# A graph-network kernel on one Trainium2 core: GpSimd's second sum of weights is moved ahead of the fifth unit of row gathers

## The chip, the cores and the metric

The kernel runs on one core of one Trainium2 chip. A core has five engines that run side by side and meet at semaphores: TensorE (PE in the profile; PEld is its weight load), VectorE (DVE), ScalarE (ACT), GpSimd (POOL) and SyncE (SP, which only issues DMAs). The metric is the device time of one execution in microseconds. Before the change it is 3512.61 us, the median of 3 runs (3510.88 to 3514.73).

## The reference, cut to what matters

The program is a graph network over 1250 nodes of 768 features: two attention layers, and then a relational layer with 34 relations and 41250 edges. The part that the change touches is the relational layer:

```
agg  = segment_sum(x[src], edge_type * n + dst)        # per relation and node
mean = agg / max(cnt, 1)
h1   = sum over r of mean[r] @ W_rel[r] + x @ W_root + b_rgcn
xw   = h1 @ W_gcn          # then one more sum over the edges, a bias, a layer norm
```

The kernel turns the order round: it first computes `y[r] = x @ W_rel[r]` for all relations, stores these rows in DRAM, and then gathers for each edge the row `y[type, src]`, scales it by 1/count and adds it up per destination node.

## The kernel before, in words

The output columns are computed in two halves of 384 (`q` is 0 or 1; the name `y_half` in the profile is the store in DRAM). In each half 17 steps go over two relations at a time. The products of a step are made by a scheme with seven block products in place of eight (`m1` to `m7`), for 5 tiles of nodes each: 35 slots of 9 f16 matmuls of 128x384 (lines L2424, L2426, L2427). It needs four sums of weight blocks in each step, all made on GpSimd from the loaded weights, each a TENSOR_TENSOR of 128x1152:

- the first (`t3`, L792): X1 = B22 - B12, as soon as the next step's weights have landed;
- the second (`t1`, L798): B12 = B12 - B11, in place, after VectorE has measured B11 and B12 (the wait on `w_max`);
- the third (`t2`, L800): X2 = B22 - B12, after the second;
- the fourth (`t4`, L806): B11 = B21 - X2, at the start of the next step, after VectorE's `low` of product 1 (L1799).

In the second half (`q` = 1) fifteen of the steps also sum the edges of the first half, six units of 512 edges a step, numbered 0 to 5. For each unit

- GpSimd's `gather` issues four indirect DMAs (L840) of 128 rows of y. They need the row buffers free, of which there are two sets, so unit c's gathers wait (`e_lo`) for VectorE's rows of unit c - 2, two of them at a time;
- ScalarE's `edge_high` (L1213) scales the four sets of rows and rounds them;
- VectorE's `edge_low` makes for each set a one-hot matrix (L1838) and the rest of the rounding (L1840);
- TensorE's `edge_sum` multiplies them (L2400, L2401, eight matmuls), and VectorE's `edge_add` (L1861) adds the result up.

Every engine's order within a step is written out by hand in its `one_step` or `rows_step`. TensorE runs m1, m7, unit 0, m6, m2, m5 (first tile), unit 1, the rest of m5, m4, m3, unit 2, then tiles 2 and 3 of m1 and m7 and tile 2 of m6, unit 3, tile 3 of m6, m2, the largest weight (`spread_max`), m5, m4, unit 4, m3, and tile 4 with unit 5. VectorE measures the next step's weights (L1764) just ahead of `edge_low` of unit 3, then stands `edge_add` of unit 2, then `edge_low` of unit 4, then the additions for m2 and `scale`. The outputs of the products leave PSUM by ScalarE (L1238) and VectorE (L1875).

On GpSimd a step of the loop (`rows_step`) is: fourth sum, gathers of units 1, 2, 3, first sum, gathers of units 4 and 5, second and third sum, gathers of unit 0 of the next step (in the code: unit `PER`). The loop runs 14 times, and a fifteenth step stands behind it without the last gathers.

Of the kernel before, what the change touches and what calls it, by code (L numbers as in the profile page):

```python
# [19 lines left out]
def program(nc, x, src, dst, etype, norm_g, norm_b, W1, a_src1, a_dst1, b1, W2, a_src2, a_dst2, b2,  # L20
# [32 lines left out]
    with ctx:  # L53
# [484 lines left out]
        def step(q, i):  # L538
            return i + q * PAIRS


        def unit(q, i, m, c):

            return i * m + (c + q * UNITS), c % 2, i * (m // 2) + (c // 2 + q * (UNITS // 2) + W_USES[0])
# [208 lines left out]
        def _(pool):  # L753
# [34 lines left out]
            def t3(q, i):  # L788

                for j in range(2):  # L790
                    pool.wait_ge(w_loaded[j], step(q, i) * 16 + 16)
                nc.gpsimd.tensor_tensor(X1, B22, B12, ALU.subtract).then_inc(t_done, 1)  # L792

            def t1_t2(q, i):

                pool.wait_ge(w_max, step(q, i) * 5 + 2)
                pool.wait_ge(t_done, step(q, i) * 4 + 1)
                nc.gpsimd.tensor_tensor(B12, B12, B11, ALU.subtract).then_inc(t_done, 1)  # L798
                pool.wait_ge(t_done, step(q, i) * 4 + 2)
                nc.gpsimd.tensor_tensor(X2, B22, B12, ALU.subtract).then_inc(t_done, 1)  # L800

            def t4(q, i):

                pool.wait_ge(w_lo_ready, step(q, i) * 7 + LOW[1])
                pool.wait_ge(t_done, step(q, i) * 4 + 3)
                nc.gpsimd.tensor_tensor(B11, B21, X2, ALU.subtract).then_inc(t_done, 1)  # L806
# [25 lines left out]
            def gather(q, i, m, c):  # L832

                V, place, _ = unit(q, i, m, c)
                pool.wait_ge(idx_next, V + 1)
                for t in range(UT):
                    if t % FREE == 0:
                        pool.wait_ge(e_lo, V * UT + (t + FREE))
                        pool.nop(nofuse=True)
                    nc.gpsimd.indirect_dma_start(  # L840
                        out=graw[place * UT + t], out_offset=None, in_=y_dram[q],
                        in_offset=bass.IndirectOffsetOnAxis(ap=idx_now[:, c % IDXB, t:t + 1], axis=0))\
                        .then_inc(g_loaded[place * UT + t], 16)
# [20 lines left out]
            pool.wait_ge(o2_ones, 1)  # L864
            t3(0, 0)
            t1_t2(0, 0)
            t4(0, 0)
            pool.wait_ge(idx_copied, 1)
# [6 lines left out]
            pool.wait_ge(x1_lo, 7 * HT)  # L875
            t3(0, 1)
            t1_t2(0, 1)

            def weights_step(q, i, next_q, next_i, b):

                t4(q, i)
                pool.wait_ge(idx_copied, i + 1)
                pool.nop(nofuse=True)
                weigh(b, 0)
                weigh(b, 1)
                t3(next_q, next_i)
                weigh(b, 2)
                weigh(b, 3)
                t1_t2(next_q, next_i)
                weigh(b, 4)  # L890
                weigh(b, 5)

            def rows_step(q, i, e, next_q, next_i, last=False):

                t4(q, i)
                gather(q - 1, e, PER, 1)
                gather(q - 1, e, PER, 2)
                gather(q - 1, e, PER, 3)
                t3(next_q, next_i)
                gather(q - 1, e, PER, 4)  # L900
                gather(q - 1, e, PER, 5)
                t1_t2(next_q, next_i)
                if not last:
                    gather(q - 1, e, PER, PER)

# [16 lines left out]
            with pool.Fori(0, AGG_PAIRS - 1) as i:  # L922
                rows_step(1, i + 1, i, 1, i + 2)
            rows_step(1, AGG_PAIRS, AGG_PAIRS - 1, 1, AGG_PAIRS + 1, True)
            plain_step(1, PAIRS - 1, HALVES, 0)
            t4(HALVES, 0)
# [1801 lines left out]
```

## Time and profile before

| What | us |
|---|---|
| Median of 3 runs | 3512.61 (3510.88 to 3514.73) |
| Span of the profiled execution, first to last instruction | 3486.4 |
| Median less span: what lies around the span | 26.2 |
| TensorE busy | 3187.3 (91% of the span) |
| VectorE busy | 2289.5 (66%) |
| GpSimd busy | 1672.5 (48%) |
| ScalarE busy | 1477.8 (42%) |
| The fifteen steps with row gathers, from fourth sum to fourth sum | 918.46 |

The profiled execution's time with what lies around its span is not told apart from the runs; the 26.2 us are taken for it. Busy time of TensorE is a union of modelled matmul times (0.33 us for a matmul that is started every 0.16 us), so a pause under 0.17 us does not show in it; the length of a step does.

### The profile page before, as it was taken

To read this page: it belongs to the slowest core of one execution; us is meant where nothing else is said; L and a number is where in the kernel's file an instruction comes from. 1 tells how busy PE (TensorE), PEld (TensorE's weight loads), DVE (VectorE), ACT (ScalarE), POOL (GpSimd) and SP (SyncE) were. 2 spreads that over 40 slices of the span, in tenths; PEclk is the share of its full clock that TensorE was granted. 3 is DMA by queue.
4 is the path that set the end of the run, shared out by engine and by line. 5 is a ranking of instruction groups with operands and counts; after the bars stand their busy time and mean duration, and the time that the engine had idled before them with its cause. 6 is when DMAs were issued, how large, how long until landed. Compare 5 with 4: busy or idle time off the path is not lost.

```text
span 3486.4 us, 59747 instructions
## 1 busy us (share of the span) xinstructions
PE 3187.3 (91%) x17307; PEld 1981.5 (57%) x17307; DVE 2289.5 (66%) x4661; ACT 1477.8 (42%) x2713; POOL 1672.5 (48%) x1373
## 2 busy tenths in 40 slices
PE   6989998987999999999999999999999998678888
PEld 4544458976555555555556666666666654333545
DVE  8989988869744544454556877878788754432335
ACT  3767757645433323233343545545455531110010
POOL 3720000003566666656414565665656536766653
PEclk9999999998999999999999999999999998889899
DMA  3020012021423233232335564555556534664442
GB/s 91 2 73 0 0 55 79 1 87 59 152 90 124 97 116 120 103 124 98 124 104 170 172 199 155 194 164 178 187 169 198 152 127 130 192 178 136 133 111 80
DMA packets 228626, 411.91 MB, mean 118 GB/s; under 512 B 37764, under 2 KB 177923, under 8 KB 228534
## 3 DMA queue, kind: packets, MB, share of 16 engines
q1 hardware_dynamic: 167664, 268.22, 21.9%
q0 software_dynamic: 60480, 142.01, 15.2%
q8 instruction: 54, 0.88, 0.1%
q10 hardware_dynamic: 390, 0.50, 0.1%
q14 instruction: 38, 0.31, 0.0%
HBM read 259.19 MB, written 151.32 MB: 118 GB/s over the span
## 4 chain that ended last, share of the span: by engine, by line
PE 71%; DVE 12%; issue 7%; POOL 3%; another core or an unknown queue 3%; ACT 2%; DVEq 1%; DMA 1%; ACTq 0%; POOLq 0%
PE bank L2427 17%; PE bank L2424 17%; PE bank L2426 16%; PE bank L2413 6%; POOL placed_dram L778 3%; DVE arena L1635 3%; PE bank L2266 2%; PE bank L2400 2%; PE bank L2401 2%; PE bank L2326 2%; PE bank L2671 2%; DVE arena L1692 2%; DVE arena L1730 2%; DVE arena L1634 1%
## 5 line engine op out<-in xcount | busy, mean ns | idle before, releaser
L2424 PE MATMUL bank<-arena 128*128 128x384 f16 x3675 | 1205.3, 328 | 59.5 <-ACT arena L1238 38.2
L2427 PE MATMUL bank<-arena 128*128 128x384 f16 x3675 | 1204.2, 328 | 6.3 <-issue 6.2
L2426 PE MATMUL bank<-arena 128*128 128x384 f16 x3675 | 1203.9, 328 | 4.7 <-issue 4.6
L1238 ACT ACTIVATE arena<-bank,winv 128x384 f32<-128x384 f32 x700 | 395.7, 578 | 973.1 <-PE bank L2427 813.3
L1875 DVE SCALAR_TENSOR_TENSOR arena<-bank,winv,arena 128x384 f32<-128x384 f32 x525 | 313.9, 613 | 399.0 <-PE bank L2427 362.3
L2424 PEld LDWEIGHTS bank<-arena 128*128 128x128 f16 x3675 | 360.9, 98 | 324.4 <-ACT arena L1238 46.2
L2427 PEld LDWEIGHTS bank<-arena 128*128 128x128 f16 x3675 | 361.0, 98 | 248.6 <-issue 13.8
L2426 PEld LDWEIGHTS bank<-arena 128*128 128x128 f16 x3675 | 361.4, 98 | 238.6 <-issue 14.9
L1799 DVE SCALAR_TENSOR_TENSOR arena<-arena,wscale 128x1152 f16<-128x1152 f32 x245 | 367.8, 1536 | 193.7 <-ACT arena L1171 177.3
L840 POOL DMA_INDIRECT arena<-y_half,idx_now x360 | 395.1, 1097 | 190.1 <-issue 101.9
L854 POOL DMA_INDIRECT arena<-y_half,idx_now x360 | 351.8, 977 | 185.1 <-issue 106.1
L2413 PE MATMUL bank<-arena 128*128 128x384 f32 x720 | 281.9, 539 | 70.5 <-issue 45.3
L1861 DVE TENSOR_TENSOR arena<-arena,bank 128x384 f32 x180 | 99.3, 552 | 299.6 <-remote 139.8
L1171 ACT ACTIVATE arena<-arena,wscale 128x1152 f16<-128x1152 f32 x245 | 294.9, 1245 | 1.9 <-DVE wscale L1786 1.5
L863 POOL MEMSET arena<- 1x1250 f32 x1 | 1.1, 1136 | 604.9 <-DVE arena L1715 604.9
L1213 ACT ACTIVATE agg_hi<-arena,typ_s 128x384 fp32r<-128x384 f32 x360 | 192.4, 607 | 171.4 <-PE bank L2401 151.6
L2413 PEld LDWEIGHTS bank<-arena 128*128 128x128 f32 x720 | 145.8, 210 | 192.3 <-issue 101.9
L1840 DVE SCALAR_TENSOR_TENSOR agg_lo<-arena,typ_s,agg_hi 128x384 fp32r<-128x384 f32 x360 | 237.9, 661 | 12.5 <-ACT agg_hi L1213 10.2
L2212 PE MATMUL bank<-arena 128*128 128x512 f16 (+1 forms) x1080 | 212.9, 346 | 25.0 <-DVE arena L1635 18.4
L806 POOL TENSOR_TENSOR arena<-arena 128x1152 f32<-128x1152 f32 x35 | 92.2, 2634 | 292.7 <-DVE arena L1799 292.7
L827 POOL DMA_INDIRECT w_now<-rel_inv_dram,idx_now x192 | 198.9, 1036 | 54.7 <-issue 51.5
L792 POOL TENSOR_TENSOR arena<-arena 128x1152 f32<-128x1152 f32 x35 | 92.2, 2635 | 239.7 <-DMA arena<-in_L_gnn_W_rel_dram 216.8
(269 smaller groups left out, 4611.5 us busy)
## 6 DMA issues: line engine op xcount, KB each, us to landing
y_half<-arena SPq DMA_DIRECT2D x306, 384.0 KB
arena<-in_L_gnn_W_rel_dram SPq DMA_DIRECT2D x68, 1152.0 KB
arena<-y_half,idx_now POOLq DMA_INDIRECT x720
y_half<-arena SPq DMA_DIRECT2D x34, 294.0 KB
cT_dram<-arena SPq DMA_DIRECT2D x1, 5625.0 KB
arena<-cT_dram SPq DMA_DIRECT2D x9, 625.0 KB
arena<-in_x_dram SPq DMA_DIRECT2D x10, 384.0 KB, 9.0
xu_dram<-arena SPq DMA_DIRECT2D x9, 384.0 KB
```

The lines of the kernel that those rows point to most:

```text
L840: nc.gpsimd.indirect_dma_start(out=graw[place * UT + t], out_offset=None, in_=y_dram[q], in_offset=bass.IndirectOffsetOnAxis(ap=idx_now[:, ...
L854: nc.gpsimd.indirect_dma_start(out=tail_rows[k], out_offset=None, in_=y_dram[HALVES - 1], in_offset=bass.IndirectOffsetOnAxis(ap=idx_now[: ...
L1171: nc.scalar.activation(by_rel(w_hi[m - 1]), block, ACT.Copy, scale=wscale[:, 0:1]).then_inc(w_hi_ready, 1)
L1238: nc.scalar.activation(y[half][:, :, c * CQ:(c + 1) * CQ], acc, ACT.Copy, scale=scale).then_inc(r_copied, 1)
L1799: nc.vector.scalar_tensor_tensor(by_rel(w_lo[m - 1]), block, wscale[:, 0:1], by_rel(w_hi[m - 1]), ALU.mult, ALU.subtract).then_inc(w_lo_re ...
L1840: nc.vector.scalar_tensor_tensor(agg_lo[:, t, :], graw[place * UT + t], w_s[:, at], agg_hi[:, t, :].bitcast(F32), ALU.mult, ALU.subtract). ...
L1875: nc.vector.scalar_tensor_tensor(to, acc, winv[:, 0:1], to, ALU.mult, ALU.add).then_inc(r_added, 1)
L2212: ins = nc.tensor.matmul(bank[j][:, 0:hi - lo], oh_d[:, jj * UT + t, :], oh_s[:, jj * UT + t, lo:hi], start=False, stop=False, skip_group_ ...
L2413: nc.tensor.matmul(acc, tail_oh[place * UT + t], tail_rows[k], start=(t == 0), stop=(t == UT - 1))\
L2424: nc.tensor.matmul(acc, h, w_hi[m - 1][:, k, :], start=fresh and k == 0, stop=False, skip_group_check=True)
L2426: nc.tensor.matmul(acc, h, w_lo[m - 1][:, k, :], start=False, stop=False, skip_group_check=True)
L2427: ins = nc.tensor.matmul(acc, l, w_hi[m - 1][:, k, :], start=False, stop=k == KH - 1, skip_group_check=True)
```

## The change

The function `t1_t2`, which made the second and the third sum, is split in two, `t1` and `t2`. In `rows_step`, which is used by the fifteen steps with row gathers alone, `t1` now stands between the gathers of units 4 and 5, and `t2` where both stood. All other callers still make both in a row. No wait, no operand and no size is changed.

```diff
-            def t1_t2(q, i):
+            def t1(q, i):
 
                 pool.wait_ge(w_max, step(q, i) * 5 + 2)
                 pool.wait_ge(t_done, step(q, i) * 4 + 1)
                 nc.gpsimd.tensor_tensor(B12, B12, B11, ALU.subtract).then_inc(t_done, 1)
+
+            def t2(q, i):
+
                 pool.wait_ge(t_done, step(q, i) * 4 + 2)
                 nc.gpsimd.tensor_tensor(X2, B22, B12, ALU.subtract).then_inc(t_done, 1)
+
+            def t1_t2(q, i):
+
+                t1(q, i)
+                t2(q, i)
@@
                 t3(next_q, next_i)
                 gather(q - 1, e, PER, 4)
+                t1(next_q, next_i)
                 gather(q - 1, e, PER, 5)
-                t1_t2(next_q, next_i)
+                t2(next_q, next_i)
```

GpSimd's instructions in the loop of the second half, from the first sum (L792) to the gathers of the next step's unit 0, in the kernel before; L840 are the gathers, two at a time, L798 and L800 the second and third sum:

```order
L792 TENSOR_TENSOR arena<-arena 128x1152
L835 REGISTER_ALU
L838 ISA
L840 DMA arena<-y_half,idx_now 128x384 x2
L838 REGISTER_ALU
L840 DMA arena<-y_half,idx_now 128x384 x2
L835 REGISTER_ALU
L838 ISA
L840 DMA arena<-y_half,idx_now 128x384 x2
L838 REGISTER_ALU
L840 DMA arena<-y_half,idx_now 128x384 x2
L796 ISA
```

Eight gathers stand in a row, and the first instruction of the second sum's waits (L796) comes behind them. In the changed kernel the same place reads (L848 are the gathers, L798 is still the second sum, L803 the third):

```order
L848 DMA arena<-y_half,idx_now 128x384 x2
L796 ISA
L797 ISA
L798 TENSOR_TENSOR arena<-arena 128x6x192
L843 REGISTER_ALU
L846 ISA
L848 DMA arena<-y_half,idx_now 128x384 x2
L846 REGISTER_ALU
L848 DMA arena<-y_half,idx_now 128x384 x2
L802 REGISTER_ALU
L803 TENSOR_TENSOR arena<-arena 128x1152
```

The first row is the second pair of unit 4's gathers. The second sum has moved ahead of unit 5's four gathers, which now stand alone between two sums; the third sum keeps its place.

## Rows read from the trace of the kernel before

**Rows 1.** The page, part 4: the chain that ended last, by engine.

```profile
PE 71%; DVE 12%; issue 7%; POOL 3%; another core or an unknown queue 3%; ACT 2%; DVEq 1%; DMA 1%; ACTq 0%; POOLq 0%
```

**Rows 2.** Busy time by stretch: the fifteen steps, fourth sum to fourth sum.

```profile
core 0: us, PE busy (x) PEld busy (x) DVE busy (x) ACT busy (x) POOL busy (x), PEclk, DMA share, GB/s
1866.46:1925.67 59.21, 58.08 (x355) 37.31 (x354) 50.60 (x88) 31.36 (x57) 35.88 (x28) 1.00 0.57 186
...
2172.72:2234.52 61.80, 60.33 (x367) 39.12 (x365) 48.40 (x90) 31.49 (x58) 37.43 (x28) 1.00 0.55 177
...
2602.40:2662.29 59.89, 59.89 (x367) 39.03 (x365) 51.01 (x90) 31.94 (x58) 37.34 (x28) 1.00 0.56 182
...
sum 918.46, PE 903.29 PEld 582.82 DVE 733.27 ACT 474.63 POOL 551.20; mean PE 60.22 PEld 38.85 DVE 48.88 ACT 31.64 POOL 36.75
```

**Rows 3.** GpSimd in order of time: start, us, what, count, idle before and releaser.

```profile
2172.72 2.63 POOL L806 TENSOR_TENSOR arena<-arena 128x1152 f32<-128x1152 f32 x1 [6.86 <-DVE arena L1799]
2175.50 1.90 POOL L840 DMA_INDIRECT arena<-y_half,idx_now  x1
...
2200.55 2.64 POOL L792 TENSOR_TENSOR arena<-arena 128x1152 f32<-128x1152 f32 x1 [3.04 <-DMA arena<-in_L_gnn_W_rel_dram]
...
2207.10 1.13 POOL L840 DMA_INDIRECT arena<-y_half,idx_now  x1 [0.30 <-issue]
2208.53 1.15 POOL L840 DMA_INDIRECT arena<-y_half,idx_now  x1 [0.30 <-issue]
...
2213.44 2.63 POOL L798 TENSOR_TENSOR arena<-arena 128x1152 f32<-128x1152 f32 x1
2216.15 2.62 POOL L800 TENSOR_TENSOR arena<-arena 128x1152 f32<-128x1152 f32 x1
2220.69 0.98 POOL L840 DMA_INDIRECT arena<-y_half,idx_now  x1 [1.92 <-DVE agg_lo L1840]
```

**Rows 4.** VectorE in the same step: end of unit 3, start of unit 4.

```profile
2208.24 0.61 DVE L1840 SCALAR_TENSOR_TENSOR agg_lo<-arena,typ_s,agg_hi 128x384 fp32r<-128x384 f32 x1
2215.14 1.02 DVE L1838 TENSOR_SCALAR agg_oh<-iota,dst_s 128x128 fp32r<-128x128 f16 x1 [5.82 <-PE bank L2401]
2216.95 2.24 DVE L1840 SCALAR_TENSOR_TENSOR agg_lo<-arena,typ_s,agg_hi 128x384 fp32r<-128x384 f32 x1 [0.78 <-ACT agg_hi L1213]
```

**Rows 5.** TensorE in the same step, unit 3's sums and the slot behind.

```profile
2211.25 0.47 PE L2400 MATMUL bank<-agg_hi,agg_oh 128*128 128x384 f32 x1
...
2212.58 0.33 PE L2401 MATMUL bank<-agg_lo,agg_oh 128*128 128x384 f32 x1 [0.17 <-issue]
2213.30 0.33 PE L2400 MATMUL bank<-agg_hi,agg_oh 128*128 128x384 f32 x1 [0.38 <-issue]
...
2214.72 0.32 PE L2424 MATMUL bank<-arena 128*128 128x384 f16 x1 [0.92 <-issue]
```

**Rows 6.** ScalarE in the same step.

```profile
2214.80 1.52 ACT L1238 ACTIVATE arena<-bank,winv 128x384 f32<-128x384 f32 x3 [3.75 <-remote]
```

**Rows 7.** GpSimd in the step that begins at 2602.40.

```profile
2638.54 0.96 POOL L840 DMA_INDIRECT arena<-y_half,idx_now  x1 [1.56 <-DVE agg_lo L1840]
...
2643.28 2.64 POOL L798 TENSOR_TENSOR arena<-arena 128x1152 f32<-128x1152 f32 x1
2645.99 3.02 POOL L800 TENSOR_TENSOR arena<-arena 128x1152 f32<-128x1152 f32 x1
```

**Rows 8.** VectorE in the step that begins at 2602.40, unit 4.

```profile
2641.72 0.33 DVE L1838 TENSOR_SCALAR agg_oh<-iota,dst_s 128x128 fp32r<-128x128 f16 x1 [2.04 <-issue]
2642.54 0.62 DVE L1840 SCALAR_TENSOR_TENSOR agg_lo<-arena,typ_s,agg_hi 128x384 fp32r<-128x384 f32 x1 [0.49 <-ACT agg_hi L1213]
2643.07 2.93 DVE L1838 TENSOR_SCALAR agg_oh<-iota,dst_s 128x128 fp32r<-128x128 f16 x1
...
2646.46 2.63 DVE L1838 TENSOR_SCALAR agg_oh<-iota,dst_s 128x128 fp32r<-128x128 f16 x1
```

**Rows 9.** GpSimd in the step that begins at 1866.46, unit 4 to unit 5.

```profile
1901.36 0.96 POOL L840 DMA_INDIRECT arena<-y_half,idx_now  x1 [1.88 <-DVE agg_lo L1840]
```

## The prediction

> **What bounds the kernel now.** First the page's chain of waits: TensorE holds 71% of it, GpSimd 3% [rows 1]. So GpSimd's own time is worth nothing; a move on it counts only through what it does to TensorE. Then the busy times by stretch for the fifteen steps that the change touches [rows 2]. They last 918.46 us together. The reader is to see that TensorE is busy nearly all of each step (60.33 of 61.80 us in the one that begins at 2172.72), at full granted clock (1.00), and that one step, the one at 2602.40, did the same number of matmuls (367) in 59.89 us without a pause. The first, at 1866.46, took 59.21. The other thirteen took 918.46 - 59.21 - 59.89 = 799.36 us, 61.49 each. This kernel can thus run the step 1.60 us faster than it mostly does, and the whole room that the change has is about 13 x 1.60 = 20.8 us, 0.6% of the kernel. Everything outside these steps is untouched.
>
> Next, in order of time, where the 1.60 us go. In the step at 2172.72 TensorE starts unit 3's sums at 2211.25 and then pauses three times, 0.17, 0.38 and 0.92 us, until 2214.72 [rows 5]. At the same moment ScalarE ends a wait of 3.75 us (2214.80, releaser "remote", three evictions at once) [rows 6] and VectorE one of 5.82 us (2215.14) [rows 4]. ScalarE's three evictions were of slots that TensorE had started well before. So three engines stand still together and start together at 2214.7 to 2215.1, and the profile names no instruction that they waited for. I don't know the mechanism. What I see is its place: GpSimd has just ended eight gathers without a break. The first of unit 5 starts 0.30 us behind the last of unit 4 (2207.10 + 1.13 to 2208.53), and the last ends where the second sum starts, at 2213.44 [rows 3]. The standstill ends 1.3 us after that.
>
> In the fast step at 2602.40 the first gather of unit 5 stood 1.56 us behind unit 4's last, since it waited for VectorE [rows 7], and VectorE began unit 4 after a wait of 2.04 us only [rows 8]. In the other fast step, at 1866.46, that break was 1.88 us [rows 9]. In none of the thirteen slow steps was there a break over 0.5 us at this place. Two of two fast steps with the break, none of thirteen slow ones: that is the ground of this forecast, and it is a coincidence in time, not yet a cause.
>
> **The change, part by part.** No instruction is added or removed: fifteen second sums of 2.63 us stand elsewhere. GpSimd's work from the first sum to the third is as long as before.
>
> *Second sum, earlier.* Its wait for the measured weights is over by then: VectorE measures before it starts unit 3's rows, and it is in the last row of unit 3 at 2208.24 [rows 4], the moment when unit 4's gathers end (2208.23). So it starts there, about 5.2 us earlier than 2213.44, and makes the break between the gathers 0.3 + 2.63, about 3 us, twice the 1.56 of the fast step.
>
> *The same sum beside VectorE.* In the slow step the second and third sum lie on VectorE's unit 4. An L1838 of 0.28 us took 1.02 and ended with the second sum, an L1840 of 0.6 took 2.24 and ended 0.4 behind the third [rows 3, 4]; in the fast step two L1838 took 2.93 and 2.63 us [rows 8]. So a sum on GpSimd holds up such a VectorE instruction for up to its own 2.63 us. In the new place the second sum meets the end of unit 3: the last L1840 (2208.24 to 2208.85) can be held to 2208.24 + 2.63 + 0.61 = 2211.5. TensorE begins unit 3 at 2211.25 and reads the last row at the seventh of eight matmuls, 0.17 us apart, near 2212.3. So this costs 0 while there are 0.8 us of cover. In a step where the sum starts half a microsecond earlier, the row before is held too, and the last is ready at about 2211.9: still covered.
> The Trainium skill, SBUF — State Buffer, section "Who interferes with whom", says that a VectorE instruction with two SBUF inputs contends with a GpSimd instruction that reads SBUF, and that whoever issues first holds the shared ports for the whole instruction. By that rule, the trace agrees (2.24 and 2.93 us above), and the rule speaks against this change: it is the mechanism of the slower rival below.
>
> *Unit 4 on VectorE.* It now meets the third sum alone, and if it starts at 2211.9 + 0.3, as in the fast step relative to TensorE, it is almost through before the third sum begins. The 2.3 to 2.6 us that VectorE no longer loses lie ahead of the additions for m2 and `scale`, which TensorE reaches later; in a few of the thirteen steps TensorE still paused 0.2 to 0.6 us ahead of unit 4's sums. I count that inside the 1.60.
>
> *Gathers of unit 5.* They start about 2.7 us later (2208.5 to 2211.2) and run beside VectorE's unit 4. Beside VectorE's rows a gather can take 1.90 us in place of 0.95 [rows 3], so four of them may take 5 to 8 us. Cover: ScalarE needs these rows only 15 us later, behind unit 4. Price 0.
>
> *Third sum.* It follows them at 2216 to 2219, against 2216.15 before. Its result is used after VectorE's `low`, and the fourth sum in the next step waited 6.86 us for VectorE anyway [rows 3]. Unit 0's gathers waited 1.92 us for VectorE. Price 0 up to 2 us of delay.
>
> **The sum.** The unknown term is how much of the standstill goes. Upper end: all thirteen steps become like the one at 2602.40, -20.8 us. Nearest case on the other side: the standstill stays as it is, 0 us. I take the upper end's row, since the break of 3 us in each step is longer than either of the two that went with a fast step, less a little for steps in which something else is late next (0.1 us each): 13 x 1.5 = 19.5 us. The profiled execution then has a span of 3486.4 - 19.5 = 3466.9; with the 26.2 us around it, by which its span stands below the median of the runs, that is 3493.1.
>
> **The rivals.** A change under 0.2%, 7 us, is what a measurement of this kernel can't tell from none.
>
> *The standstill moves along.* It may belong to how much the DMA queues carry (stores, weights and gathers come together here), not to the run of eight gathers, or a VectorE that is late may be the cause of the break and of the fast step. For: ScalarE's "remote" releaser, and no GpSimd instruction that anyone waits for. Against: the thirteen to two. Then unit 5's gathers, 2.7 us later, bring it back 2.7 us later at the same price. Left is the second sum's hold on VectorE, 0 to 0.3 us a step: 3508 to 3513, same.
>
> *Half of it goes.* The break splits eight gathers in two fours, but the third sum begins right behind the second four, and the pause shrinks from 1.6 to 0.8: 13 x 0.8 = 10 us, 3502, faster.
>
> *Slower: unit 3's last rows come late.* If GpSimd gets its sum in ahead of the third of the four rows, or the sum starts 1 us earlier than reckoned, row 4 is ready at 2207.6 + 2.63 + 3 x 0.73 = 2212.4 and more, up to 0.8 us behind TensorE's need, in each of fifteen steps: +12 us on top of a standstill that stays, 3525. It decides from the point where the sum starts before the second row of unit 3 is done. Against it: unit 4's gathers would have to end 0.7 us sooner than in rows 3. With a standstill that goes it would only eat half of the gain.
>
> *The change doesn't do what it says*: the second sum waits for the measurement and holds unit 5's gathers. Excluded up to 2 us of delay: the measurement is done before unit 3's first row. Beyond that, as the rival before.
>
> **How the numbers follow.** The standstill gone, 3493 (3487 to 3499): 0.47. Half gone, 3502: 0.16. Moved along, 3511: 0.22. Slower, 3525: 0.15. So faster by over 0.2% 0.62, within 0.2% 0.23, slower 0.15. The range leaves out the last tenth at the slow side and goes a little under the upper end of the sum (the first step, at 59.21, was faster still; fifteen such steps would give 3482): 3485 to 3519.
>
> **What would show it.** In the profile after: the second sum starts within 0.1 us of unit 4's last gather and 2.7 us before unit 5's first; the steps last 59.5 to 60.2 us; no wait of 3 us or more on ScalarE and VectorE that end together with a pause of TensorE behind unit 3. Wrong: steps still at 61 us with the common start now at about 2217 by the clock of rows 3 (the standstill moved), or TensorE waiting for L1840 inside unit 3's eight matmuls (the slower rival), or VectorE's unit 3 rows held with no pause on TensorE and steps unchanged.

## The result and the profile after

The changed kernel takes 3482.77 us, the median of four runs (3474.68 to 3485.73), against 3511.86 for the kernel before beside it (3510.88 to 3514.73): ratio 0.991, 95% interval 0.9889 to 0.9932, or 29 us less. The forecast was 3493. The direction and the place of the gain were right; the time came out 2.2 us below the low end of the range, 3485.

The kernel before takes 3346 to 3350 us in some series of runs and 3489 to 3514 us in others (short and long executions below), so every kernel below is compared only with runs of the kernel before in its own series.

The fifteen steps of the changed kernel, busy time by stretch (columns as in [rows 2]):

```profile
core 0: us, PE busy (x) PEld busy (x) DVE busy (x) ACT busy (x) POOL busy (x), PEclk, DMA share, GB/s
1874.01:1933.22 59.21, 58.08 (x355) 37.31 (x354) 48.58 (x88) 31.16 (x57) 36.03 (x28) 1.00 0.57 186
...
2172.77:2232.66 59.89, 59.89 (x367) 39.02 (x365) 49.93 (x90) 31.54 (x58) 37.22 (x29) 1.00 0.57 182
...
sum 897.90, PE 896.67 PEld 583.62 DVE 741.48 ACT 474.37 POOL 559.35; mean PE 59.78 PEld 38.91 DVE 49.43 ACT 31.62 POOL 37.29
```

The reader is to see that the step which took 61.80 us in [rows 2] takes 59.89, as the one at 2602.40 did, and that TensorE is busy through all of it. The sum went from 918.46 to 897.90, which is 20.6 us less of the 20.8 that the prediction had called all the room there is.

GpSimd in the step at 2172.77, in order of time (columns as in [rows 3]; the second sum is now L798, the third L803, the gathers L848):

```profile
2207.41 0.95 POOL L848 DMA_INDIRECT arena<-y_half,idx_now  x1 [0.30 <-issue]
2208.38 2.63 POOL L798 TENSOR_TENSOR arena<-arena 128x1152 f32<-128x1152 f32 x1
2211.17 1.30 POOL L848 DMA_INDIRECT arena<-y_half,idx_now  x1 [0.16 <-issue]
...
2215.32 1.14 POOL L848 DMA_INDIRECT arena<-y_half,idx_now  x1 [0.31 <-issue]
2216.48 2.63 POOL L803 TENSOR_TENSOR arena<-arena 128x1152 f32<-128x1152 f32 x1
2219.27 0.96 POOL L848 DMA_INDIRECT arena<-y_half,idx_now  x1 [0.16 <-issue]
```

The second sum starts 0.02 us behind unit 4's last gather and 2.79 us ahead of unit 5's first. The third sum starts 0.3 us later than in [rows 3], and unit 0's gathers, which waited 1.92 us for VectorE there, now wait for nothing and start 1.4 us earlier.

VectorE at the same place (L1847 and L1849 are L1838 and L1840 of before):

```profile
2207.59 0.61 DVE L1849 SCALAR_TENSOR_TENSOR agg_lo<-arena,typ_s,agg_hi 128x384 fp32r<-128x384 f32 x1
2208.12 2.98 DVE L1847 TENSOR_SCALAR agg_oh<-iota,dst_s 128x128 fp32r<-128x128 f16 x1
2211.02 0.61 DVE L1849 SCALAR_TENSOR_TENSOR agg_lo<-arena,typ_s,agg_hi 128x384 fp32r<-128x384 f32 x1
```

The sum on GpSimd holds VectorE's last L1847 of unit 3 for 2.98 us, until just behind the sum's own end (2208.38 + 2.63 = 2211.01), and the last row is ready at 2211.63. TensorE and ScalarE around it:

```profile
2211.31 0.47 PE L2409 MATMUL bank<-agg_hi,agg_oh 128*128 128x384 f32 x1
...
2212.66 0.34 PE L2410 MATMUL bank<-agg_lo,agg_oh 128*128 128x384 f32 x1
2212.84 0.34 PE L2433 MATMUL bank<-arena 128*128 128x384 f16 x1
```

```profile
2209.36 1.52 ACT L1247 ACTIVATE arena<-bank,winv 128x384 f32<-128x384 f32 x3 [2.98 <-PE bank L2436]
2211.64 0.58 ACT L1247 ACTIVATE arena<-bank,winv 128x384 f32<-128x384 f32 x1 [0.76 <-PE bank L2436]
```

TensorE reads the held row with its last two matmuls, at 2212.49 and 2212.66, 0.9 us after it is ready: no pause where [rows 5] had three. ScalarE's evictions still come three at once at 2209.36, but there is no releaser "remote" and no common start of three engines. VectorE's L1849 takes 613 ns on average over the kernel, where L1840 took 661:

```profile
L1849 DVE SCALAR_TENSOR_TENSOR agg_lo<-arena,typ_s,agg_hi 128x384 fp32r<-128x384 f32 x360 | 220.8, 613 | 10.3 <-ACT agg_hi L1222 7.9
```

One of the fifteen steps is different, the one at 2591.98, which takes 60.25 us. There the second sum starts 34.5 us into the step, where it starts 35.6 us into the step at 2172.77, and so it meets VectorE's first row of unit 3 and not its last. GpSimd, VectorE and TensorE:

```profile
2626.47 2.63 POOL L798 TENSOR_TENSOR arena<-arena 128x1152 f32<-128x1152 f32 x1
...
2625.87 3.32 DVE L1847 TENSOR_SCALAR agg_oh<-iota,dst_s 128x128 fp32r<-128x128 f16 x1
...
2631.29 0.61 DVE L1849 SCALAR_TENSOR_TENSOR agg_lo<-arena,typ_s,agg_hi 128x384 fp32r<-128x384 f32 x1
...
2631.52 0.33 PE L2410 MATMUL bank<-agg_lo,agg_oh 128*128 128x384 f32 x1
2631.95 0.44 PE L2409 MATMUL bank<-agg_hi,agg_oh 128*128 128x384 f32 x1
```

All four rows of unit 3 are about 3 us late by this hold (3.32 us for an instruction of 0.29). The fourth is ready at 2631.90, and TensorE's seventh matmul starts right behind it, at 2631.95, 0.43 us after the sixth and not 0.17. This step is 0.36 us longer than 59.89.

### The profile page after: what moved, and what is told of

Its sections match the earlier page's. It is cut to its first block, busy times and chain, and to the rows that moved or that the text cites. A ratio compares the mean times of both kernels' runs of the same rounds, so it can differ in the third digit from the quotient of the medians.

```text
span 3478.1 us, 59747 instructions
## 1 busy us (share of the span) xinstructions
PE 3183.8 (92%) x17307; PEld 1981.8 (57%) x17307; DVE 2288.0 (66%) x4661; ACT 1475.2 (42%) x2713; POOL 1681.9 (48%) x1373
## 4 chain that ended last, share of the span: by engine, by line
PE 70%; DVE 12%; issue 7%; POOL 3%; another core or an unknown queue 3%; ACT 2%; DVEq 1%; DMA 1%; ACTq 0%; POOLq 0%
PE bank L2436 17%; PE bank L2433 17%; PE bank L2435 17%; PE bank L2422 5%; POOL placed_dram L778 3%; DVE arena L1644 3%; PE bank L2275 2%; PE bank L2680 2%; PE bank L2335 2%; PE bank L2410 2%; PE bank L2409 2%; DVE arena L1701 2%; DVE arena L1739 2%; DVE arena L1643 1%
## 5 line engine op out<-in xcount | busy, mean ns | idle before, releaser
L848 POOL DMA_INDIRECT arena<-y_half,idx_now x360 | 405.2, 1126 | 167.3 <-issue 100.6
L862 POOL DMA_INDIRECT arena<-y_half,idx_now x360 | 353.9, 983 | 189.1 <-issue 107.4
L1849 DVE SCALAR_TENSOR_TENSOR agg_lo<-arena,typ_s,agg_hi 128x384 fp32r<-128x384 f32 x360 | 220.8, 613 | 10.3 <-ACT agg_hi L1222 7.9
L792 POOL TENSOR_TENSOR arena<-arena 128x1152 f32<-128x1152 f32 x35 | 92.2, 2634 | 238.9 <-DMA arena<-in_L_gnn_W_rel_dram 216.1
```

The costliest lines, as they stand in the source:

```text
L848: nc.gpsimd.indirect_dma_start(out=graw[place * UT + t], out_offset=None, in_=y_dram[q], in_offset=bass.IndirectOffsetOnAxis(ap=idx_now[:, ...
L862: nc.gpsimd.indirect_dma_start(out=tail_rows[k], out_offset=None, in_=y_dram[HALVES - 1], in_offset=bass.IndirectOffsetOnAxis(ap=idx_now[: ...
L1849: nc.vector.scalar_tensor_tensor(agg_lo[:, t, :], graw[place * UT + t], w_s[:, at], agg_hi[:, t, :].bitcast(F32), ALU.mult, ALU.subtract). ...
```

## The experiments

The theory going in: a run of eight gathers without a break on GpSimd is what the standstill hangs on, and the change gains by breaking it. The rivals: it is not the break but the earlier second sum (VectorE's unit 4 meets one sum less), or the bytes that the gathers move, or no property of the order at all. The kernel before, the changed kernel and four further versions are to tell them apart. Most were run in several series, since in many series the kernel before has no standstill. In the expectations of `break_only` and `early_sum`, "theory A" is the run of eight, "B" VectorE's unit 4, and "C" how late unit 5 is issued.

**The kernel before, again.**

> The kernel before, unchanged, to get a second profile of it: the profiled execution of before had a span of 3486.4 us, while its runs took 3511 to 3515 us. Theory A (the fifteen steps lose more in a usual execution than in the one profiled): a span near 3510, with the fifteen steps near 940 us in place of 918.5. Theory B (what differs lies outside these steps): a span near 3510 with the fifteen steps at 917 to 921 us and the rest 24 us longer. Theory C (26 us lie around the span): the span again near 3486 and the time near 3512.

It took 3348.24 us (3341.55 to 3353.38), the runs beside it 3350.14: ratio 0.9998 (0.9988 to 1.0008). Not 3511: 163 us less for the same instructions. It was run in two more series, to find one with the standstill:

> The kernel before again, for a second profile of it on the chip where it takes 3511 us. Theory A: the fifteen steps last 925 to 945 us there, more than the 918.5 of the first profile, and the span is near 3512. Theory B: the steps last 917 to 921 us and the other 24 us lie in the first half or the tail. If it meets the chip where it takes 3350 us: 59.89 us a step, as before.

> The kernel before, for a second profile on the chip where it takes 3511 us. Theory A: the fifteen steps last 925 to 945 us there, more than the 918.5 of the first profile, span near 3510. Theory B: the steps last 917 to 921 us and the other 24 us lie outside. On a chip where it takes 3350 us: 59.89 us a step.

Both were of the short kind again: 3345.64 us (ratio 0.9996) and 3347.25 (0.9999). Its profile in the first series, first two of the fifteen steps and their sum:

```profile
1871.89:1931.78 59.89, 59.89 (x367) 39.03 (x365) 46.48 (x90) 31.96 (x58) 37.69 (x29) 1.00 0.58 182
1931.78:1991.66 59.88, 59.88 (x367) 39.03 (x365) 50.81 (x90) 31.95 (x58) 37.39 (x28) 1.00 0.58 182
...
sum 897.53, PE 896.41 PEld 583.72 DVE 741.15 ACT 478.51 POOL 556.59; mean PE 59.76 PEld 38.91 DVE 49.41 ACT 31.90 POOL 37.11
```

And GpSimd in one of them, the eight gathers in a row and the second sum behind, as before the change:

```profile
2205.65 1.19 POOL L840 DMA_INDIRECT arena<-y_half,idx_now  x1 [0.30 <-issue]
2207.14 1.15 POOL L840 DMA_INDIRECT arena<-y_half,idx_now  x1 [0.30 <-issue]
...
2211.09 0.95 POOL L840 DMA_INDIRECT arena<-y_half,idx_now  x1 [0.30 <-issue]
2212.05 2.64 POOL L798 TENSOR_TENSOR arena<-arena 128x1152 f32<-128x1152 f32 x1
```

No break (the longest of the fourteen steps behind the first is 0.68 us), and each of these steps takes 59.8 to 59.9 us. So the run of eight is not enough by itself to make a standstill. Nor do VectorE's holds by the sums on GpSimd make one: in the step of these rows they hold two instructions of unit 4 for 3.71 and 2.63 us, and the step still takes 59.89. The series differ outside the fifteen steps too: most steps of the kernel's first half take 52.1 us here and 55.3 to 56.1 in a series of 3489 us.

**Only the break, the second sum left where it was.** Eight writes of 128x128 zeros to a tile that is no longer read, 2.5 us together, between unit 4 and unit 5:

```diff
                 gather(q - 1, e, PER, 4)
+                pause(e, 8)
                 gather(q - 1, e, PER, 5)
                 t1_t2(next_q, next_i)
```

> The kernel before with a pause of eight small memsets (about 2.5 to 3.5 us together, write only, on a tile that is dead by then) between the gathers of units 4 and 5; both sums stay behind unit 5. Theory A (the standstill comes from eight gathers in a row): the steps go to 59.9 us, as in the changed kernel, total 3480 to 3492. Theory B (what helped is that the second sum no longer lies on VectorE's unit 4): the steps stay at 61.4 us or more, total 3510 or more, since both sums now lie even later.

> A pause of eight small memsets between the gathers of units 4 and 5, both sums behind unit 5. Where before takes 3511 us: theory A (run of eight) 59.9 us a step, total 3480 to 3490; theory B (the second sum beside VectorE's unit 4) 61.4 us or more, total 3510 or more. Where before takes 3350 us: no difference.

> A pause of eight small memsets between the gathers of units 4 and 5, both sums behind unit 5, meant for the chip where before takes 3511 us. Theory A (run of eight): 59.9 us a step, total 3480 to 3490. Theory B (the second sum beside VectorE's unit 4): 61.4 us or more, total 3510 or more.

> A pause of eight small memsets between the gathers of units 4 and 5, both sums behind unit 5. Where before takes 3511 us: theory A (run of eight) 59.9 us a step, total 3480 to 3490; theory B (the second sum beside VectorE's unit 4) 61.4 us or more, total 3510 or more. Where before takes 3350 us: no difference.

In these four series, in which the kernel before took 3346 to 3350 us, it changed nothing: ratios 0.9995 (0.9985 to 1.0004), 1.0003 (0.9994 to 1.0013), 1.001 (1.0 to 1.002) and 1.0002 (0.9991 to 1.0013). They say nothing on the standstill, for there was none to remove; they show that the break costs nothing. The fifth series was of the other kind:

> A pause of eight small memsets between the gathers of units 4 and 5, both sums behind unit 5. Where before takes 3511 us: theory A (run of eight) 59.9 us a step, total 3480 to 3490; theory B (the second sum beside VectorE's unit 4) 61.4 us or more, total 3510 or more. Where before takes 3350 us: no difference.

3467.22 us (3463.26 to 3468.0) against 3488.72: ratio 0.9931 (0.9911 to 0.995), 21.5 us less. Its steps, and GpSimd in one of them (the gathers are L851, the second sum L799, the third L801):

```profile
1921.81:1982.31 60.50, 60.50 (x371) 39.33 (x369) 48.60 (x90) 32.45 (x59) 39.42 (x37) 1.00 0.58 180
...
sum 897.57, PE 896.43 PEld 583.47 DVE 706.43 ACT 477.00 POOL 581.30; mean PE 59.76 PEld 38.90 DVE 47.10 ACT 31.80 POOL 38.75
```

```profile
2255.36 0.94 POOL L851 DMA_INDIRECT arena<-y_half,idx_now  x1 [0.30 <-issue]
2256.30 2.49 POOL L811 MEMSET tri<- 128x128 f32 x8
2259.47 0.95 POOL L851 DMA_INDIRECT arena<-y_half,idx_now  x1 [0.69 <-issue]
...
2264.23 2.64 POOL L799 TENSOR_TENSOR arena<-arena 128x1152 f32<-128x1152 f32 x1
2266.95 2.62 POOL L801 TENSOR_TENSOR arena<-arena 128x1152 f32<-128x1152 f32 x1
```

Both sums stand side by side behind unit 5, as before the change, and the fifteen steps still take 897.57 us, TensorE busy in all of each but the first (the step of 60.50 holds 371 matmuls in place of 367: the boundary, the fourth sum, moved, not the work). So the gap between unit 4's and unit 5's gathers brings the whole gain of these steps; the earlier second sum is not needed for it. The gap also puts both sums 2 to 3 us later, behind VectorE's unit 4 (its last row ends at 2264.11, the second sum starts at 2264.23), so by this run alone VectorE's unit 4 could still be the cause. The order of time speaks against it: in [rows 5] TensorE's first two pauses end at 2212.58 and 2213.30, before the second sum starts at 2213.44 [rows 3].

**Only the earlier sum, the run of eight kept.** The second sum ahead of unit 4:

```diff
                 t3(next_q, next_i)
+                t1(next_q, next_i)
                 gather(q - 1, e, PER, 4)
                 gather(q - 1, e, PER, 5)
-                t1_t2(next_q, next_i)
+                t2(next_q, next_i)
```

> The second sum stands ahead of unit 4's gathers, straight behind the first sum; units 4 and 5 are gathered in one run of eight, the third sum behind them. Theory A (run of eight): the standstill stays, steps 61 to 62 us, total about 3510. Theory B (the second sum's hold on VectorE in unit 4): the steps go to 59.9 us, total about 3483. Theory C (it is how late unit 5 is issued against the stores and weights in the DMA queues): unit 5 starts about where it does in the changed kernel, so 59.9 us as under B.

> The second sum ahead of unit 4's gathers; units 4 and 5 in one run of eight, then the third sum. Where before takes 3511 us: theory A (run of eight) steps of 61 to 62 us, total about 3511; theory B (the second sum beside VectorE's unit 4) or C (how late unit 5 is issued) 59.9 us, total about 3483. Where before takes 3350 us: no difference.

> The second sum ahead of unit 4's gathers; units 4 and 5 in one run of eight, then the third sum, meant for the chip where before takes 3511 us. Theory A (run of eight): steps of 61 to 62 us, total about 3511. Theory B (the second sum beside VectorE's unit 4) or C (how late unit 5 is issued): 59.9 us, total about 3483.

> The second sum ahead of unit 4's gathers; units 4 and 5 in one run of eight, then the third sum. Where before takes 3490 or 3511 us: theory A (run of eight) steps of 61 to 62 us, total as before within 5 us; theory B (the second sum beside VectorE's unit 4) or C (how late unit 5 is issued) 59.9 us, 20 us or more below before. Where before takes 3350 us: no difference.

In these four series of 3346 to 3350 us: 0.9996 (0.9987 to 1.0006), 0.9995 (0.9985 to 1.0004), 1.0001 (0.9991 to 1.0011), 0.9996 (0.9985 to 1.0008), so nothing. In the last series, where it stood beside the kernel before once more:

> The second sum ahead of unit 4's gathers; units 4 and 5 in one run of eight, then the third sum. Where before takes 3490 or 3511 us: theory A (run of eight) steps of 61 to 62 us, total as before within 5 us; theory B or C (the second sum off VectorE's unit 4, or how late unit 5 is issued) 59.9 us, 20 us or more below before. Where before takes 3350 us: no difference.

> The kernel before, for a second profile on a chip where it takes 3490 or 3511 us: A, the fifteen steps last 918 to 945 us and carry what the change gained (20 to 29 us over 59.9 us each); B, they last 917 to 921 us even in an execution of 3511 us, and what the change gained beyond 20.6 us lies outside them. Where it takes 3350 us: 59.89 us a step.

The kernel before took 3489.1 us there (3487.39 to 3495.65; beside it 3488.93) and this one 3478.87 (3471.1 to 3482.38): ratio 0.9966 (0.9954 to 0.9979), 10 us less. That is neither the "within 5 us" of theory A nor the "20 us or more" of B and C. The steps of the two, the kernel before first:

```profile
2174.32:2236.47 62.15, 60.52 (x367) 39.12 (x365) 48.39 (x90) 31.49 (x58) 36.98 (x28) 1.00 0.55 176
...
sum 921.46, PE 904.29 PEld 582.89 DVE 732.71 ACT 474.27 POOL 551.63; mean PE 60.29 PEld 38.86 DVE 48.85 ACT 31.62 POOL 36.78
```

```profile
2109.01:2168.89 59.88, 59.88 (x367) 39.03 (x365) 47.67 (x90) 32.29 (x58) 37.23 (x28) 1.00 0.58 182
...
2230.26:2291.64 61.38, 60.23 (x367) 38.86 (x365) 46.77 (x90) 31.86 (x58) 36.83 (x28) 1.00 0.55 178
...
sum 911.34, PE 900.56 PEld 582.35 DVE 711.45 ACT 479.42 POOL 551.10; mean PE 60.04 PEld 38.82 DVE 47.43 ACT 31.96 POOL 36.74
```

921.46 - 911.34 = 10.1 us, as much as the medians differ by. Ten of the fifteen steps still have pauses and five have none. GpSimd, ScalarE and TensorE in the step at 2230.26, one with pauses:

```profile
2263.61 0.96 POOL L848 DMA_INDIRECT arena<-y_half,idx_now  x1
...
2272.53 0.95 POOL L848 DMA_INDIRECT arena<-y_half,idx_now  x1 [0.30 <-issue]
2273.50 2.63 POOL L803 TENSOR_TENSOR arena<-arena 128x1152 f32<-128x1152 f32 x1
```

```profile
2270.77 0.58 ACT L1247 ACTIVATE arena<-bank,winv 128x384 f32<-128x384 f32 x1 [3.76 <-remote]
2273.63 0.58 ACT L1247 ACTIVATE arena<-bank,winv 128x384 f32<-128x384 f32 x1 [2.27 <-PE bank L2436]
2275.14 2.13 ACT L1222 ACTIVATE agg_hi<-arena,typ_s 128x384 fp32r<-128x384 f32 x4 [0.93 <-remote]
```

```profile
2275.00 0.32 PE L2436 MATMUL bank<-arena 128*128 128x384 f16 x1 [0.76 <-issue]
...
2277.89 0.34 PE L2433 MATMUL bank<-arena 128*128 128x384 f16 x1 [0.39 <-ACT arena L1247]
```

The eight gathers end at 2273.48; ScalarE (2275.14, "remote") and TensorE (2275.00) start together 1.5 us later. In [rows 3 to 6] that was 1.3 us. It looks like the same standstill: it moved along with the run of eight and became a little smaller. But in the step at 2109.01 the same run is there without a break, and nothing pauses:

```profile
2144.33 1.30 POOL L848 DMA_INDIRECT arena<-y_half,idx_now  x1
...
2153.63 0.94 POOL L848 DMA_INDIRECT arena<-y_half,idx_now  x1 [0.30 <-issue]
2154.59 2.65 POOL L803 TENSOR_TENSOR arena<-arena 128x1152 f32<-128x1152 f32 x1
```

What differs there is its place. It begins 35.3 us into the step, where the other begins at 33.4, because the weights came later (5.45 us of waiting for them ahead of the first sum against 3.18). In all five steps without a pause unit 5's gathers begin 40.0 to 41.3 us into the step, in the ten with pauses 38.0 to 39.2. So a run of eight is neither enough (this step, and all of the kernel before in a series of 3348 us), nor is the break the only way to be rid of the pause; when the gathers come counts as well in this order. How late unit 5 is issued (theory C) doesn't decide it by itself either: the ten steps with pauses begin its gathers at 38.0 to 39.2 us, and `break_only_e`, with steps that begin them at 37.5 to 40.8, has no pause; in the kernel before the steps with pauses begin them at 35.5 to 38.1, and the step at 2602.40, which had the break, at 36.1.

**Fewer bytes in the same run.** Units 4 and 5 fetch 96 columns of 384, of other rows, so the result of these units is not the reference's:

```diff
-                        out=graw[place * UT + t], out_offset=None, in_=y_dram[q],
+                        out=graw[place * UT + t][:, 0:96] if few else graw[place * UT + t], out_offset=None,
+                        in_=y_few[q] if few else y_dram[q],
```

> The kernel before with units 4 and 5 gathering rows of 96 in place of 384 columns (other rows than the reference's, so the sums of these edges are left out in effect); the same number of gathers at the same places. Theory A1 (what counts is the bytes in the DMA queues): the standstill goes, steps 59.9 us, total about 3485. Theory A2 (what counts is the run of eight descriptor-making instructions on GpSimd): the standstill stays, steps 61.4 us, total about 3511.

> Units 4 and 5 gather rows of 96 in place of 384 columns of y (other rows, so these edges' sums are left out in effect), order of before. Where before takes 3511 us: theory A1 (bytes in the DMA queues) 59.9 us a step, about 3485; theory A2 (the run of eight instructions on GpSimd) 61.4 us, about 3511. Where before takes 3350 us: no difference.

3348.55 us beside 3350.14, ratio 0.9998 (0.9988 to 1.0008), and in a second series 3346.04 beside 3348.58, 0.9998 (0.9988 to 1.0008). Neither series had a standstill to remove, so whether bytes or the number of gathers counts stays open. What they do show: with no standstill, a quarter of the bytes of a third of the gathers is worth nothing.

**The changed kernel again, and the same idea in the first half.**

> The changed kernel, unchanged. On a chip where the kernel before runs its gather steps in 59.89 us already (as in before_again: 3348 us): theory S (the change is worth exactly the standstill, and where there is none it is worth nothing) expects the same time as before within 0.1%. Rival: the second sum's new place is worth something by itself (VectorE's unit 4 is free earlier), 0.3 us a step, 4 us or 0.12%. On a chip where before takes 3511 us, both expect 3475 to 3486 us.

3485.57 us (3483.45 to 3487.48) against 3514.26: ratio 0.9921 (0.9903 to 0.9939). The result repeats. Its fifteen steps take 897.79 us.

The other kernel is the changed one with the second sum also moved in the first half's order:

```diff
                 weigh(b, 2)
+                t1(next_q, next_i)
                 weigh(b, 3)
-                t1_t2(next_q, next_i)
+                t2(next_q, next_i)
                 weigh(b, 4)
```

> The changed kernel with the same idea in the first half: second sum after the third weight-gather unit, third sum after the fourth, so that the 16 + 8 small gathers of a step no longer stand in runs of 8 ahead of and behind both sums. Theory S: where the first half's steps take 52.1 us (no standstill), no change. On a chip with the standstill (first-half steps of 55.6 to 56.4 us), it goes from part of fourteen steps: -10 to -40 us against the changed kernel. Rival: no gain there, since a run of 12 gathers stands behind the third sum.

3476.28 us (3473.81 to 3477.39) against the same 3514.26: ratio 0.9895 (0.9878 to 0.9912), 9.3 us below the changed kernel beside it, and so the best version measured. Its reason is not the expected one: fifteen steps of the first half take 834.0 us together against 835.2, and thirteen of them still 55.6 to 57.2 us each. Of the 9.7 us between the two spans (3472.1 and 3481.8), 7.8 are there when the third step of that half begins (979.1 us against 986.9), and 4.4 of these already at the first fourth sum (839.1 against 843.5), which stands ahead of the changed loop; over all twenty profiles that sum starts at 838.6 to 843.5. So 4.4 us are not the edit's, and whether the rest is its gain isn't shown: two executions of the changed kernel differ by 3.7 us in span.

## Why the prediction was right or wrong

**The view of the bound, and the room.** Right. TensorE ends the chain, GpSimd counts only by what it does to it, and 20.8 us of room were 20.6 us of gain in the profiled executions (918.46 to 897.90). The remark that the first step, at 59.21, "was faster still" is a misreading that widened the range: that step holds 355 matmuls in place of 367, and it takes 59.2 us in the changed kernel too.

**The cover of the moved sum.** Right for most steps, with another instruction held. The sum caught the last L1847 (2.98 us), not the last L1849; the row was ready at 2211.63 (forecast: up to 2211.5), and TensorE needed it near 2212.5. The slower rival, which started from an earlier sum and a late last row, is real in one step: in the one at 2591.98 it costs 0.36 us (60.14 us in place of 60.25 in `after_again`). In the other fourteen TensorE has no pause in unit 3. The Trainium skill, SBUF — State Buffer, section "Who interferes with whom", says that whoever issues first has the shared ports for the whole instruction and the other is blocked, and names `tensor_scalar`, as L1847 is, among the instructions that can take part. The trace agrees on the length of the hold (2.98 us for one that takes 0.28); which of the two was first it doesn't tell, since L1847's record begins 0.26 us ahead of the sum's. The prediction put its 2.93 us under the rule for two SBUF inputs, but that was an L1838, a `tensor_scalar` of one tensor; only its 2.24 us were of a two-input instruction.

**VectorE, unit 4, the gathers of unit 5 and the third sum.** Right. The four gathers of unit 5 took 5.3 us where 5 to 8 were reckoned, the third sum started at 2216.48 (reckoned: 2216 to 2219), and TensorE waited for none of them.

**How much of the standstill goes.** Nearly right: all of it, 1.58 us of 1.60 for a step, where 1.5 was taken. The rivals "moves along" and "half of it goes" are out for this order; but `early_sum_f` shows both outcomes for another order: the standstill moved with the run of eight in ten steps, and 10 of the 24 us over 897.5 went, most of it in five steps that lost the pause.

**The cause, "eight gathers without a break".** Half right. The break gives the whole gain (`break_only_e`, 21.5 us), so it was a sound guide to the edit. The prediction's count was a little off: two of its thirteen slow steps had breaks over 0.5 us (0.61 in the step at 1987.23, shown here, and 0.68 in the one at 2357.21).

```profile
2022.75 0.96 POOL L840 DMA_INDIRECT arena<-y_half,idx_now  x1 [0.61 <-issue]
```

The pattern held in the later profiles of long executions, five steps of `early_sum_f` aside. `before_f` has fourteen steps with breaks of 0.69 us at most, all slow, and one with 1.79, which takes 59.89. Over the seven profiles of long executions the 63 steps with a break of 1.56 us or more have no such pause, and of the 42 without one 37 do. As a sufficient cause the run of eight falls: the kernel before has the run of eight and no standstill in any series of 3348 us, and five steps of `early_sum_f` do in a series of 3489.

**The sum: the step that failed is "with the 26.2 us around it".** The prediction took a span of 3486.4 from one execution and a median of 3512.61 from others and called the difference what lies around the span. What lies around the span is 1.7 to 3.1 us in every run on record (the changed kernel: 3479.96 us with a span of 3478.1; the kernel before in its last profile: 3491.34 and 3489.6). The profiled execution of before was thus one of 3488 to 3490 us, of the kind of the series at 3489, while the timed runs were of 3511. So executions of two kinds were mixed. Against the 3489 us of its own kind the forecast of -19.5 us would have given 3469.5, and `break_only_e` in such a series measured 3467.22, -21.5. Against 3511.86 the gain was 29 us, not 19.5. The 8 to 9 us by which this exceeds the 20.6 of the profiled steps are in no trace: no execution of the kernel before of 3511 us was profiled. Whether its fifteen steps are longer than 918 to 921 us or other parts shrank with the change stays open. What `after_again` shows outside the steps can't settle it: its first half's loop takes 835.2 us and the part behind the steps 656.3, where the kernel before in a series of 3489 has 830.1 and 648.2, but `break_only_e`, in such a series too, has 828.5 and 653.1, so part of the longer tail comes with the break itself.

That 3493 came within 10 us of the measured time is partly luck: the forecast span of 3466.9 was 11 us too short for this kind of execution (3478.1), and the term of 26.2 us was some 24 us too long.

The range was set from the bounds of the pauses alone (its low end a little under the full room, 3485). A bound for the time around the span, which no row of the trace gave, was missing; with next to nothing as that bound the range would have reached to about 3467.

## What to carry to other kernels

Before a forecast is put on a median, compare the profiled execution's span with it: a gap of more than the few us that lie around a span (1.7 to 3.1 here) means that the profile is of another kind of execution than the timed runs, and both the base and the size of the effect are then uncertain by that gap. A pause that ends on three engines at once, with no releaser in the profile, can be worth an edit even when its mechanism is unknown: here 2.5 us of other work between two blocks of gathers took away about 1.6 us in each of thirteen steps. Try such an edit in more than one series of runs, since in another one (3348 us) it is worth nothing.

## What the runs showed of the hardware

One program, three levels: 3345 to 3350, 3489 and 3511 to 3514 us, stable to 0.3% within a series; the same chip gave 3345.54 and 3488.72 for the kernel before in two series. TensorE's granted clock is 1.00 in the fifteen steps of both, so it is not behind their pauses. Over the span it is 0.983 against 0.967, and lower in the first half, where there are pauses too (0.98 against 1.00 from 985 to 1814 us); which of the two follows from the other there isn't shown. The long executions lose time not only here: in `before_f` the first half's steps with gathers take 55.9 us where they take 52.09 in `before_again`, and the part behind the steps 648 where it takes 581. What both losses share is that GpSimd issues gathers there. Steps without gathers take the same in both: 52.2 and 52.2 us against 52.1 and 52.2 for the last two of the first half, and 52.97 in both for the one behind the fifteen; up to the first fourth sum it is 842.4 against 840.4.

The traces of long executions also lack a part of their records. The weights' transfers carry a time to landing in all thirteen profiles of short executions and in none of the seven of long ones. First the line of the DMA issues in `before_again`, then in `before_f`:

```profile
arena<-in_L_gnn_W_rel_dram SPq DMA_DIRECT2D x68, 1152.0 KB, 8.1
```

```profile
arena<-in_L_gnn_W_rel_dram SPq DMA_DIRECT2D x68, 1152.0 KB
```

Counted over the whole trace, 36359 semaphore updates are recorded in `before_again` and 21732 in `before_f`, for the same 59747 instructions; nine in ten of the missing ones are DMA completions. So a releaser "remote" or "issue" in a long execution can also mean that the record of the releaser is missing. Folded over the second to the fifteenth step, the first 8 us of a step have 39 and 36 of them; from 32 to 40 us into it, just ahead of the standstill and at the end of the stretch in which most DMA packets are recorded (about 2,900 from 20 to 36 us in both), there are 132 and 40. But the changed kernel (67) and `break_only_e` (71) lack half of them there too and don't pause, so lost records and the standstill don't go together step by step. The Trainium skill, NOTIFIC — the notification-queue block, section "7.1 Overflow: three behaviours, one of which stalls the engine", says that the internal pipeline of the block that writes such records always holds up its producers rather than lose a record. The records that are missing here must then be lost elsewhere, which no run explains. A hold-up would make a standstill of three engines with no releaser, right after a burst of records, and could explain why a short gap in the gathers removes it. It isn't shown: no run here was made without recording, or with fewer records, and whether the long executions are long for that reason is the question that stays open.
